# The transposed x of a Mamba pair in two banks, multiplied by dt in two halves, with the gate's projection behind the first

## What is computed

```python
proj = hidden_states @ in_proj_w
gate, hbc, dt = proj[..., :4096], proj[..., 4096:8448], proj[..., 8448:]
hbc = silu(causal_conv4(hbc) + conv_b)          # -> x, B, C
dt = softplus(dt + dt_bias)
cum = cumsum(dt * A)                            # within a chunk
Y_diag = (C @ B.T * decay) @ (x * dt)
states = (decay_states * B).T @ (x * dt)        # carried from chunk to chunk
Y_off = state_decay * (C @ prev_states)
y = (Y_diag + Y_off + D * x) * silu(gate)
out = rms_norm(y) * norm_w @ out_proj_w
```

## Time and profile before

| | |
|---|---|
| median of 3 runs | 2059.26 us (2057.95 to 2059.41) |
| the profiled execution's own time | 2056.03 us |
| its span, first to last instruction | 2053.5 us |
| busy: PE, PEld, DVE, ACT, POOL | 1955.8, 1588.7, 1449.0, 1302.5, 833.4 us |
| mean granted TensorE clock | 0.988 |
| DMA over the span | 231.00 MB, 112 GB/s |

### The profile page before, as it was taken

One profiled execution on the slowest core, in us unless ns is written; L12 is line 12 of the kernel. 1 busy time (PEld: TensorE's weight loads), 2 busy tenths in 40 slices (PEclk: granted clock), 3 DMA queues, 4 the chain that ended last, 5 costly groups with the idle time before them and its releaser, 6 DMA issues.

```text
span 2053.5 us, 42545 instructions
## 1 busy us (share of the span) xinstructions
PE 1955.8 (95%) x12684; PEld 1588.7 (77%) x12684; DVE 1449.0 (71%) x2472; ACT 1302.5 (63%) x2978; POOL 833.4 (41%) x1000
## 2 busy tenths in 40 slices
PE   5999999999999999999989999999999999999998
PEld 4888678778788857878778885778878888588786
DVE  4775568888677457888857745888876773588886
ACT  3663279999555237888835523888874551488885
POOL 2120158888300015677620001677671000176776
PEclk9999999999999999999989999999999999999999
DMA  5330236566222013444422201444442220144442
GB/s 197 116 115 24 90 129 204 185 203 204 93 83 81 31 44 129 148 151 145 144 63 82 82 21 44 139 151 144 146 137 80 78 68 21 59 149 148 151 144 78
DMA packets 119115, 231.00 MB, mean 112 GB/s; under 512 B 10448, under 2 KB 48528, under 8 KB 118928
## 3 DMA queue, kind: packets, MB, share of 16 engines
q1 hardware_dynamic: 119056, 230.26, 34.2%
HBM read 194.05 MB, written 36.18 MB: 112 GB/s over the span
## 4 chain that ended last, share of the span: by engine, by line
PE 70%; issue 20%; DVE 6%; POOL 2%; ACT 1%; DVEq 0%; DMA 0%; POOLq 0%; ACTq 0%
PE bank L654 30%; PE bank L892 11%; PE bank L879 6%; PE bank L859 4%; DVE place L1454 4%; PE bank L851 2%; PE bank L782 2%; PE bank L774 2%; PE bank L754 2%; PE both L774 2%; PE both L654 2%; PE bank L796 1%; PE both L754 1%; PE bank L724 1%; PE bank L729 1%
## 5 line engine op out<-in xcount | busy, mean ns | idle before, releaser
L654 PE MATMUL bank<-xn_r,w_r 128*128 128x512 f32 x2304 | 630.7, 414 | 40.0 <-DVE place L1454 29.0
L654 PEld LDWEIGHTS bank<-xn_r,w_r 128*128 128x128 f32 x2304 | 426.1, 192 | 155.9 <-issue 68.8
L1313 DVE SCALAR_TENSOR_TENSOR conv_acc<-bank,conv_sb,conv_acc 128x511 f32<-128x511 f32 (+2 forms) x408 | 304.2, 746 | 48.9 <-ACT conv_acc L1074 15.2
L533 POOL TENSOR_TENSOR rstd<-var_eps,minus_half 128x4 f32<-128x4 f32 (+2 forms) x12 | 9.7, 807 | 663.6 <-DVE var_eps L1260 663.6
L1010 ACT ACTIVATE place_r<-bank 128x512 fp32r<-128x512 f32 (+1 forms) x320 | 158.0, 556 | 158.2 <-PE bank L654 130.3
L892 PE MATMUL bank<-wo_n,place 128*128 128x256 f32 x1024 | 255.1, 392 | 1.6 <-DVE place L1438 1.6
L1247 DVE TENSOR_TENSOR place_r<-bank,place_r 128x512 fp32r<-128x512 f32 (+1 forms) x320 | 186.5, 631 | 90.3 <-ACT place_r L1010 90.3
L554 POOL TENSOR_TENSOR shared<-shared,c_t 128x768 f32<-128x768 f32 x128 | 234.5, 1832 | 0.0
L892 PEld LDWEIGHTS bank<-wo_n,place 128*128 128x128 f32 x1024 | 184.0, 189 | 42.9 <-issue 21.2
L576 POOL TENSOR_TENSOR sumsq<-sumsq,place 128x512 f32<-128x512 f32 x128 | 163.6, 1278 | 107.6 <-ACT place L1063 107.6
L654 PE MATMUL bank<-place_r 128*128 128x512 f32 (+3 forms) x960 | 193.6, 342 | 9.3 <-DVE place_r L1247 6.8
(11 more groups left out here) (154 smaller groups left out, 3493.0 us busy)
## 6 DMA issues: line engine op xcount, KB each, us to landing
place_r<-cum_rows SPq DMA_DIRECT2D x128, 512.0 KB, 3.8
w_r<-pair_split SPq DMA_DIRECT2D x96, 512.0 KB, 3.7
w_r<-qkv_split SPq DMA_DIRECT2D x48, 512.0 KB, 4.0
pair_split<-w_r SPq DMA_DIRECT2D x32, 512.0 KB, 4.1
qkv_split<-w_r SPq DMA_DIRECT2D x16, 768.0 KB, 3.8
w_r<-qkv_split SPq DMA_DIRECT2D x48, 256.0 KB, 3.2
wo_n<-out_split SPq DMA_DIRECT2D x96, 128.0 KB, 3.5
raw<-in_w_pair SPq DMA_DIRECT2D x32, 256.0 KB, 3.9
```

Source lines behind the costliest of these rows:

```text
L654: ins = mm(out, lhsT=w(a), rhs=m(b), start=(start and i == 0), stop=(stop and i == 2), **kw)
L1313: stt(out=conv_acc[:, back:W], in0=src[:, 0:W - back], scalar=conv_sb[:, ch, TAPS - 1 - back:TAPS - back], in1=conv_acc[:, back:W], op0=AL ...
```

## The change

The two first transposes go to bank 0, the two others to bank 2, each couple with an increment of its own. VectorE multiplies each couple by dt in an instruction of its own; the first increments a new semaphore, `s_xdt_half`, the second the old one. `project_gate`, which writes bank 0 alone, waits for the new one; so does the first projection of the next batch's attention. `in_block` and POOL's weigh_x still wait for `s_xdt_ready`.

```diff
             def project_gate(b, n, par):
                 pe.wait_ge(s_gate_ready, b * NPAIR + n + 1)
-                pe.wait_ge(s_xdt_ready, b * NPAIR + n + 1)
+                pe.wait_ge(s_xdt_half, b * NPAIR + n + 1)
                 project(bank[0][:], par, 0).then_inc(s_w_used, 1)
...
-                for t in range(NT):
-                    ins = pe.transpose(bank[0][:, t * P:(t + 1) * P], xs[:, par, t * P:(t + 1) * P], ident[:])
-                ins.then_inc(s_x_turned, 1)
+                for bk, t0 in ((0, 0), (2, 2)):
+                    for t in (t0, t0 + 1):
+                        ins = pe.transpose(bank[bk][:, t * P:(t + 1) * P], xs[:, par, t * P:(t + 1) * P], ident[:])
+                    ins.then_inc(s_x_turned, 1)
...
                     if not more and not last:
-                        pe.wait_ge(s_xdt_ready, (b + 1) * NPAIR + 1)
+                        pe.wait_ge(s_xdt_half, (b + 1) * NPAIR + 1)
...
-                    dve.wait_ge(s_x_turned, N + 1)
-                    tt(x_dt[:, par, :, :].rearrange("p t (h q) -> p t h q", h=2),
-                       bank[0][:].rearrange("p (t h q) -> p t h q", t=NT, h=2),
-                       dt_sb[:, :, bass.ds(n * 2, 2)].unsqueeze(3).to_broadcast([P, NT, 2, HD]), ALU.mult).then_inc(s_xdt_ready, 1)
+                    for half, (bk, t0) in enumerate(((0, 0), (2, 2))):
+                        dve.wait_ge(s_x_turned, N * 2 + half + 1)
+                        tt(x_dt[:, par, t0:t0 + 2, :].rearrange("p t (h q) -> p t h q", h=2),
+                           bank[bk][:].rearrange("p (t h q) -> p t h q", t=NT, h=2)[:, t0:t0 + 2, :, :],
+                           dt_sb[:, t0:t0 + 2, bass.ds(n * 2, 2)].unsqueeze(3).to_broadcast([P, 2, 2, HD]),
+                           ALU.mult).then_inc((s_xdt_half, s_xdt_ready)[half], 1)
```

More of the change, by code:

```diff
@@ L232, in two_layers @@
         s_x_turned = sem("x_turned")
+        s_xdt_half = sem("xdt_half")
         s_xdt_ready = sem("xdt_ready")
@@ L329, in two_layers @@
                        (s_ffn_silu, 2), (s_ffn_hid, 2), (s_y_done, 1), (s_out_ready, 2), (s_mix_ready, 1),
-                       (s_xdt_ready, 1))
+                       (s_xdt_half, 1), (s_xdt_ready, 1))
         POOL_CREDITS = ((s_squared, 1), (s_w_ready, 2), (s_stored, 16))
```

## The result

| | before | after |
|---|---|---|
| median of 4 runs | 2059.34 us (2057.95 to 2059.98) | 2032.12 us (2029.76 to 2036.26) |
| the profiled execution's own time | 2056.03 us | 2029.76 us |
| its span | 2053.5 us | 2028.0 us |
| busy PE, DVE | 1955.8, 1449.0 us | 1951.2, 1457.5 us |
| mean granted clock of TensorE | 0.988 | 0.987 |

The ratio is 0.9871, with a 95% interval of 0.9856 to 0.9887: 27 us less, with 23 to 30 in the interval. Forecast were 31 less.

A forecast was written before the change was run, and what follows sets the result against it. TensorE plus the exposed wait for x_dt was taken to bound the pairs; 7.85 us saved per batch, 31.4 in four, taken as 31, put the median at 2028 us from 2059.3, range 2016 to 2044.

The forecast's parts named there:

- What bounds the kernel: Regular pairs, 8.03 us each: bound by TensorE plus the detour through VectorE's x_dt, partly hidden by off_block.
- The wait goes, with a margin: Gate's projection: may go 0.92 us after the transposes start, 0.24 us before off_block lets it; no wait left.
- 0.26 us a pair: off_block to gate on TensorE: 1.06 us with the wait, 0.80 without; a pair falls from 8.03 to 7.77 us.
- The sum: Whole kernel: 7.85 us saved per batch, 31.4 in four batches, taken as 31 us; nothing changes outside the pairs.
- The whole stall, 0.42: Rival at the gate: the whole stall, weight-load fill included, is won back, 0.42 us a pair, 2009 us; chance 0.08.
- What it adds on VectorE: x_dt in each pair: two instructions of 424 ns replace one of 693, 0.155 us more.
- Cover for base, weigh_x and in_block: Steps after x_dt in a pair: later halves stay covered, base at most 0.1 us late, make_states with 0.1 to 0.3 left.
- ScalarE in batch 0: Nearest other bound: ScalarE's round in batch 0 is 7.61 us, below 7.77, so TensorE keeps the bound by 0.16.
- TensorE's waits at pair 0: Sign in the profile: TensorE's wait for x_dt falls from 29.0 us to about 8, the four of 2.17 shortened.
- Slower: Rival: VectorE becomes the bound, each half costing nearly a whole; 0.14 us more a pair, 2075 us; chance 0.06.
- no effect: Rival: the gate still waits, its first instruction also needing something that comes later; 2059 us; chance 0.04.
- part of it: Rival: x_dt's second half is late, make_states or in_block waits 0.1 to 0.15 us; half the gain, 2044; chance 0.14.

The follow-up runs named there:

- The third cut: The changed kernel with the second half of x_dt cut once more, into two of 128x128; 2030.65 us, ratio 0.9866.

## Why the prediction was right

- *What bounds the kernel.* Right. TensorE is without idle time through the loops, and the two ways to free it that differ most (a half-wait, another bank) end at the same 7.81 us.
- *The wait goes, with a margin.* Right. The first half starts at T+0.36 as forecast. The margin ends where it was put, near T+1.16: with the first half done at T+1.02 (started as late as before) the gate still starts 0.80 to 0.81 us after off_block, and with the second at T+1.12 and both awaited it starts about 0.10 later.
- *0.26 us a pair.* The mechanism is right and this term was mis-sized; it is 0.22 (8.03 to 7.81). "1.06 - 0.80" priced the way from off_block to the gate, and took the gate's own length as given. The stalled gate had got its first weight load out 0.03 us ahead of its first matmul (866.41, and 866.44 in the earlier trace rows):

```profile
866.41 1.22 PEld L654 LDWEIGHTS bank<-xn_r,w_r 128*128 128x128 f32 x6 [0.39 <-issue]
```

It was 1.46 us long to the next group; without the stall it is 1.49. Of 1.06 - 0.80 = 0.26 these 0.03 go off, and 0.01 is rounding.
- *The sum.* 31.4 us were added up and the profiled spans differ by 25.5. The loops' pairs gave 4.5 us less than forecast. Pair 1 gave 0.4 for 0.8, and pair 30 nothing for 0.4: there the wait for conv_end, behind it, grew from 0.78 to 0.89 us in batch 1. Pair 0 gave 3.8 for 1.1; in batches 2 and 3, at a like clock, it gave 0.32 and 0.27 as forecast (0.27), and the surplus of 2.7 is that in batches 0 and 1 it met the lower clock before and not after. And 3.3 were lost outside the pairs, which was put at nothing. That this loss and pair 0's surplus nearly cancel is luck.
- *The whole stall, 0.42.* Fell, as weighed: behind off_block the load still comes 0.17 us after the last one, and with its matmul (the 859.01 of the weight load shown above, which answers to the earlier trace rows). "TensorE: Matmul & The Clock Gate" of the Trainium skill, section Back-to-back issue gap, has the loads and matmuls of a stream pipelined; in this trace that does not hold from off_block to the gate. It does hold from the gate to make_states: that group's first load starts at 860.28, its first matmul at 860.50. The last part says what sets the two apart.

```profile
860.28 0.86 PEld L861 LDWEIGHTS bank<-shared,b_sb 128*128 128x128 f32 x6
```

- *What it adds on VectorE.* The sign is right and the size too large: 0.155 us were charged, and 0.07 measured (busy 8.5 us more for 128 pairs). Of the two cases given for the second half, "follows at once" is the true one, and even that was 0.09 too late: T+1.12 for T+1.21. The second half starts before the first has ended, and the register steps between are hidden behind it, so that of what a narrower instruction costs by its duration (424 ns and not half of 693) only 0.07 us a cut shows.
- *Cover for base, weigh_x and in_block.* Right: base at T+1.40, make_states at T+2.65 (forecast 2.62).
- *ScalarE in batch 0.* Right: its pairs too take 7.81 us.
- *TensorE's waits at pair 0.* 7.2 us are left, forecast about 8.
- *Slower, no effect, part of it.* None came. The third cut was as far as VectorE was pushed.

## What to carry to other kernels

When an engine waits for a buffer to be read, ask first whether the reader and the next writer can have different buffers, one of them free at that time: here another bank for the transposed x, and the wait left out, did what two halves and a semaphore did. Price a wait by a transition between the same two kinds of groups without a wait, and then price the stalled group itself too: during a stall some of its start-up can run ahead, here 0.03 us, and that part is not won back. When a wait is taken out at a seam, look one group further on: at pair 0 the same 1.7 us stood behind it for another engine.

## What the runs showed of the hardware

- Two tensor_tensor instructions of 128x256 from PSUM, each 415 to 426 ns by its own record, take 0.76 us together, with a satisfied wait and register steps between; one of 128x512 takes 0.69 and three pieces 0.82. A cut costs 0.06 to 0.07 us on VectorE, about half of the 0.14 to 0.15 by which the durations add up.
- TensorE's first weight load of a group comes 0.17 us after the last load of off_block (weights of 64 columns, the gate's of 128), together with its matmul. This goes with the change of the weights' shape and not with the group's wait. In the changed kernel's trace the turn of neg_cum (L820), which waits for a semaphore too, and the matmuls behind it (L775) follow small matmuls with weights of the same shape, and their first loads come without a gap; within L783, where nothing is waited for, each change between 128 and 64 rows has a gap of 0.33 us, for 0.03 between loads of one shape. In the traces of both kernels no change between 64 and 128 columns or rows has less than 0.12 us between the loads. No run changes a shape to try it.

```profile
739.28 0.97 PEld L815 LDWEIGHTS bank<-c_t,b_t 128*128 128x128 f32 x8
740.17 0.47 PEld L820 LDWEIGHTS bank<-ident,place 128*128 128x128 f32 x4
740.61 0.30 PEld L775 LDWEIGHTS both<-xn_t,gw_sb 128*128 128x128 f32 x2
```
```profile
1260.36 1.05 PEld L783 LDWEIGHTS bank<-dw_sb,shared 128*128 128x128 f32 x5
1261.75 0.29 PEld L783 LDWEIGHTS bank<-dw_sb,shared 64*128 64x128 f32 x2 [0.33 <-issue]
1262.37 1.81 PEld L783 LDWEIGHTS bank<-dw_sb,shared 128*128 128x128 f32 x9 [0.33 <-issue]
```

- The stretches at the lower clock near the seams of the batches differ between executions: the two profiled executions of the changed kernel had spans of 2028.0 and 2030.3 us at 0.987 and 0.985, with pairs alike to 0.01 us.
